# One core, a recurrent kernel with a four-stage tail: the reciprocal of the gate sum is taken over a product of two batches

## The reference, cut to what matters

```python
forget_gate = sigmoid(x @ W_f.T + b_f)
input_gate  = sigmoid(x @ W_i.T + b_i)
gate_sum    = forget_gate + input_gate + 1e-8
forget_norm = forget_gate / gate_sum
input_norm  = input_gate / gate_sum
new_info    = input_norm * (x @ W_h.T + b_h)
log_ret     = log(forget_norm + 1e-8)          # then a cumulative product over time,
hidden      = ...                              # and two cumulative sums that use it
```

## Time and profile before

| | |
|---|---|
| runs shown | 985.35, 986.1, 988.47 us, median 986.1 |
| the profiled execution | span 989.0 us (the page gives no other time of it) |
| PE busy | 943.0 us, 95% of the span |
| PEld busy | 766.4 us, 77% |
| DVE busy | 802.5 us, 81%, of which the reciprocal of the gate sum 107.3 us (32 of 3353 ns) |
| ACT busy | 647.3 us, 65% |
| POOL busy | 221.2 us, 22% |

### The profile page before, as it was taken

One profiled execution on the slowest core, in us unless ns is written; L12 is line 12 of the kernel. 1 busy time (PEld: TensorE's weight loads), 2 busy tenths in 40 slices (PEclk: granted clock), 3 DMA queues, 4 the chain that ended last, 5 costly groups with the idle time before them and its releaser, 6 DMA issues.

```text
span 989.0 us, 112546 instructions
## 1 busy us (share of the span) xinstructions
PE 943.0 (95%) x50966; PEld 766.4 (77%) x50966; DVE 802.5 (81%) x2372; ACT 647.3 (65%) x2862; POOL 221.2 (22%) x430
## 2 busy tenths in 40 slices
PE   6699999999999999999999999969999999999996
PEld 5699999999999999999999998335555555555554
DVE  2378778878788778777878787799999999999992
ACT  2478777777777777777777776336455556555552
POOL 0011111111111111111111111324434334434340
PEclk7699999999999999999999999979999999999998
DMA  6113312310010100100101001100011000001001
GB/s 218 41 55 112 110 50 95 111 35 27 24 37 24 37 24 27 34 27 24 37 24 37 24 27 33 28 1 25 24 37 34 24 24 24 24 31 41 24 24 43
DMA packets 38294, 42.01 MB, mean 42 GB/s; under 512 B 5120, under 2 KB 31232, under 8 KB 37120
## 3 DMA queue, kind: packets, MB, share of 16 engines
q1 hardware_dynamic: 36832, 40.55, 13.2%
q10 hardware_dynamic: 1440, 1.18, 0.4%
HBM read 32.80 MB, written 8.91 MB: 42 GB/s over the span
## 4 chain that ended last, share of the span: by engine, by line
PE 57%; DVE 29%; issue 7%; ACT 4%; DMA 1%; ACTq 1%; POOL 0%; DVEq 0%; POOLq 0%
PE bank L788 30%; PE bank L734 22%; DVE arena L667 10%; DVE early L686 4%; DVE early L677 4%; ACT cand_kept L391 2%; DVE early L690 2%; DVE early L684 2%; DVE early L671 2%; DVE early L665 2%; DVE none_h L604 2%; PE bank L906 2%; PE bank L923 1%; DMA bias<-in_bias 1%; PE bank L877 1%
## 5 line engine op out<-in xcount | busy, mean ns | idle before, releaser
L734 PE MATMUL bank<-x_ahead,early 128*32 128x64 f32 x12376 | 345.7, 224 | 5.9 <-ACT bank L358 3.2
L734 PEld LDWEIGHTS bank<-x_ahead,early 128*32 128x32 f32 x12376 | 239.7, 111 | 3.3 <-issue 3.3
L788 PE MATMUL bank<-none_h,early 128*32 128x32 f32 x16384 | 203.1, 199 | 8.8 <-issue 4.9
L280 POOL TENSOR_TENSOR x<-x_f,h_gx 128x64 f32 x256 | 87.6, 342 | 529.4 <-PE bank L788 528.3
L788 PEld LDWEIGHTS bank<-none_h,early 128*32 128x32 f32 x16384 | 180.6, 110 | 27.4 <-DVE none_h L604 13.5
L906 PE MATMUL bank<-x,wl 128*128 (+1 forms) x384 | 182.3, 614 | 0.9 <-DVE rank_rows L646 0.9
L788 PE MATMUL bank<-rh_f,early 128*32 128x32 f32 x8192 | 151.0, 199 | 5.0 <-DVE rh_f L592 2.2
L906 PEld LDWEIGHTS bank<-x,wl 128*128 128x128 f32 x384 | 69.2, 192 | 89.0 <-issue 89.0
L788 PEld LDWEIGHTS bank<-rh_f,early 128*32 128x32 f32 x8192 | 122.1, 112 | 7.0 <-DVE rh_f L592 5.0
L604 DVE TENSOR_TENSOR_SCAN none_h<-zero_z,cand_kept 128x64 f32<-128x64 f32 x512 | 121.6, 279 | 5.3 <-ACT cand_kept L391 3.9
L402 ACT ACTIVATE h_gx<-h_pre 128x64 f32<-128x64 f32 x256 | 68.7, 268 | 81.0 <-DVE h_pre L630 81.0
(11 more groups left out here) (95 smaller groups left out, 1294.4 us busy)
## 6 DMA issues: line engine op xcount, KB each, us to landing
x_in<-in_x SPq DMA_DIRECT2D x34, 256.0 KB, 2.7
x_ahead<-in_x SPq DMA_DIRECT2D x130, 64.0 KB, 1.8
arena<-in_w SPq DMA_DIRECT2D x8, 1024.0 KB, 5.6
out<-y SPq DMA_DIRECT2D x32, 256.0 KB, 2.5
rank_rows<-in_bias_rows SPq DMA_DIRECT2D x1, 1024.0 KB, 5.0
arena<-scratch SPq DMA_DIRECT2D x64, 16.0 KB
early<-in_cx SPq DMA_DIRECT2D x1, 768.0 KB, 4.5
early<-in_wx SPq DMA_DIRECT2D x1, 768.0 KB, 6.3
```

The costliest lines, as they stand in the source:

```text
L280: pool.tensor_tensor(x2[:, :, :, s], x1_f[:, u % LOOP], h1_gx[:, u % 2, :, :, 0], ALU.add).then_inc(x2_done, 1)
L734: mm = pe.matmul(out[32 * j:32 * j + 32], weights(k, j, m), moving(k), start=False, stop=False, tile_position=(0, 32 * j), skip_group_chec ...
L788: mm = pe.matmul(out[32 * j:32 * j + 32], weights(k, j, m), moving(k), start=False, stop=k == 1, tile_position=(0, 32 * j), skip_group_che ...
```

## The change

The reciprocal of 512 sums becomes three instructions. The sums of the two batches are multiplied with each other (256 elements), the reciprocal of the product is taken (256 elements), and that one result is multiplied with the sums again, the batches crossed over: 1/a = b * 1/(ab), and 1/b = a * 1/(ab). The last multiplication has 512 elements; it reads the sums with the two batches in reverse order, and reads the 256 inverses twice through a step of zero. Three waits of DVE on itself go between them, as there was one before.

```diff
@@ -113,6 +113,7 @@
         dec_start = sb("dec_start", [P, HALVES, GB * RUN])
+        prod, inv = [arena[2][:, 4 * COLS + n * T:4 * COLS + (n + 1) * T] for n in range(2)]
         u_s, v_s = early[:, 10 * COLS:10 * COLS + T], early[:, 10 * COLS + T:11 * COLS]
@@ -162,6 +163,7 @@
         l2_pre, f_done, i_done, c_done = sem("l2_pre"), sem("f_done"), sem("i_done"), sem("c_done")
+        prod_done, inv_done = sem("prod_done"), sem("inv_done")
@@ -664,7 +666,13 @@
                 dve.wait_ge(s_done, c + 1)
-                dve.reciprocal(rec[:, k], s_t).then_inc(rec_done, 1)
+                dve.tensor_tensor(prod, s_t[:, 0:T], s_t[:, T:COLS], ALU.mult).then_inc(prod_done, 1)
+                dve.wait_ge(prod_done, c + 1)
+                dve.reciprocal(inv, prod).then_inc(inv_done, 1)
+                dve.wait_ge(inv_done, c + 1)
+                crossed = by_batch(s_t)[:, ::-1, :]
+                both = bass.broadcast_tensor_aps(crossed, inv.rearrange("p (o t) -> p o t", o=1))[1]
+                dve.tensor_tensor(by_batch(rec[:, k]), both, crossed, ALU.mult).then_inc(rec_done, 1)
                 dve.wait_ge(rec_done, c + 1)
```

## The result

19 runs of the changed kernel took 987.25 to 992.95 us, median 991.09; 19 runs of the kernel before 985.35 to 989.35, median 986.6. The ratio is 1.0034, with a 95% interval of 1.0023 to 1.0045: 3.4 us slower, 2.3 to 4.4. One run of e5 (4792.55 us) and one of the kernel before beside it (1000.73 us) were slow and count in no ratio.

A forecast was written before the change was run, and what follows sets the result against it. PE was taken to bound the kernel at 21.26 us a phase, DVE full and in step. Start with first phase 0.6, twelve phases 1.6, lost lead 0.6 and final adapter 0.3 made +3.1: 989.2 us, range 988 to 992.

The forecast's parts named there:

- PE sets the phase and DVE's saving is worth nothing in the loop: Tail loop: PE sets 21.26 us a phase, so DVE's 0.41 us saved a unit gains nothing by itself.
- The prices of the three instructions: DVE's replacement in each unit: product of 256 at 0.43 us, reciprocal of 256 at 1.76, crossed product of 512 at 0.69.
- The pair blocks an instruction with two inputs, and which comes first behind it decides: POOL's two multiplications hold DVE's two-input instructions: the crossed product ends 0.55 us behind them, the scan starts 1.20 behind.
- The loop is 21.40 us: Loop through the engines exceeds PE's 21.26 us by 0.14; twelve such phases cost +1.6 us.
- The lost lead: End of the tail: DVE's lead over PE falls from 0.79 to 0.15 us, so the last x3 comes 0.64 later.
- The start: Start of the tail: two forget units each lose about 0.5 us net to POOL's pair, +1.0 at PE's first products.
- Half of it given back by the clock: At PE's first products, running at half clock: a microsecond less of that gives back 0.5, leaving +0.5 us.
- The final adapter: End of the kernel: PE waits longer and again starts slowly at low clock, +0.3 us, bounds -1.7 to +1.7.
- A: Rival: in the tail DVE runs ahead and the end gains, 979 to 983 us; chance 0.15.
- B: Rival: the loop closes just under PE's period, or the crossed product slips between POOL's multiplications; 987.3 us; chance 0.25.
- C: Rival: the crossed, repeated operand slows DVE's product to up to 1.4 us, 994 to 997; chance 0.12 together with D.
- D: Rival: DVE's reciprocal of 256 costs up to 3.35 us, 38 us over 32 units; chance 0.12 together with C.

The follow-up runs named there:

- e5: The kernel before, with the reciprocal taken of the first batch's 256 sums alone (work left out): 987.8 us, ratio 0.9997.
- e2: The changed kernel, with POOL's two multiplications (ic and ni) on 2 elements a partition in place of 512: 982.52 us, ratio 0.9949.
- e7: The changed kernel itself run once more, unaltered, for a second profile: 988.9 us, ratio 1.0025 to the kernel before.
- e9: The changed kernel, with six small memsets on DVE, each waited for, ahead of the first unit: 989.97 us, ratio 1.0020.
- e4: The changed kernel, with both POOL multiplications of a unit issued when the next unit's sums are ready: 989.66 us, ratio 1.0027.
- e8: The changed kernel, with the old reciprocal of 512 kept in the very first unit alone: 989.91 us, ratio 1.0024.
- e1: The kernel before, with POOL's two multiplications (ic and ni) on 2 elements a partition in place of 512: 982.41 us, ratio 0.9948.
- e3: The kernel before, with both POOL multiplications of a unit issued when the next unit's sums are ready: 981.76 us, ratio 0.9946.
- e6: The changed kernel, with only the second of POOL's two multiplications (ni) on 2 elements in place of 512: 986.34 us, ratio 0.9993.

## Why the prediction came out right, point by point

Forecast were 989.2 us, +3.1 over the median of 986.1; measured 991.09 against 986.6 in the same number of runs, ratio 1.0034 or +3.4 us (the medians, +4.5). The case in front, that the loop through PE, ACT, POOL and DVE grows past PE's own phase, is the one that happened. By its steps:

- *PE sets the phase and DVE's saving is worth nothing in the loop.* Right, and stronger than I wrote: e2 shows that the saving is worth nothing even where POOL is out of the way, and e5 that nearly four times as much is not where POOL's pair is in it.
- *The prices of the three instructions.* 0.43, 1.76 and 0.69 us against 0.42, 1.75 and 0.69 (the last in e2).
- *The pair blocks an instruction with two inputs, and which comes first behind it decides.* Right: the crossed product ends 0.54 us behind the pair, I had 0.55; L685 starts 1.19 behind, I had 1.20. By full blocking, as the prediction took it from the Trainium skill ("SBUF — State Buffer", section "Who interferes with whom"), the end would have been 0.69 behind; the rows keep some 0.14 us of overlap. The page says of two inputs that they contend, and calls the ports an exclusive lock; its words "fully blocks" stand beside DVE's 2-port modes.
- *The loop is 21.40 us.* 21.34 in the phase shown, and thirteen phases are 0.79 us longer in place of the 1.7 that I had for the loop and the first phase. This is the term that was mis-sized. Each of its links was read within 0.03 us, but what matters is the excess over 21.26, a small difference of large numbers: 0.14 forecast, 0.08 in the phase shown and 0.066 in the mean of twelve.
- *The lost lead.* 0.64 forecast, 0.72 measured. I had priced only the wait for the last x3. I had named ACT's wait for fn, but gave no term to what hangs on it: PE's second rank products come 0.73 later as well.
- *The start.* +1.0 us at PE's first products was forecast and 0.93 to 1.08 measured, but for the wrong reasons. I had each of two units lose half a microsecond to the pair. In the changed kernel the first of them loses nothing and the second 0.14; the rest, 0.94 and in e7 0.79, is the gap of 1.6 to 1.8 us before the first small reciprocal, which I had not seen coming. e9, without the gap, has the blocking that I forecast for the second unit (0.46 us).
- *Half of it given back by the clock.* The stretch behind the first rank products is 1.0 and 0.4 us shorter in the two profiles. It is not a firm term: it takes 22.66 to 23.93 us in the five profiles whose first rank products come late (the changed kernel's, e7, e4, e8, e9), and 23.71 to 24.23 in the six others.
- *The final adapter, +0.3, bounds of 1.7 either way.* Here single profiles say little. The two profiles with the change end 2.9 and 1.3 us faster than the one before; the medians say that this is chance. The stretches whose length repeats add up to 2.5 us, and 0.4 to 1.0 of that came back behind the first rank products, which leaves some 1.5 to 2.1. Where the rest of the measured 3.4 lies, the clock at the end above all or the interval of the measurement (2.3 to 4.4), isn't shown; that the sum of 3.1 came out so close is in part luck, since the phase was forecast 0.8 too dear and the gap at the start was not in it.

The rivals: that DVE runs ahead (A) is what happens without the pair or with the pair timed by DVE (e1, e2, e3), and its price was close: 979 to 983 forecast, 981.8 to 982.5 measured (5 us under the kernel before). It doesn't happen here because the crossed product is held behind the pair. The point that I named for A, M2 costing under 0.59 us behind the pair, was wrong by my own sum: 0.59 is the very value that gives the 21.40, and the loop drops under 21.26 only below 0.45. Measured are 0.58 (838.66 - 838.08), and with the measured links the point is 0.50. B, a loop just under PE's period, missed by 0.08 us. Its turned order, M2 between POOL's two multiplications, shows in the second unit of e9: M2 takes 0.73 us there, and L679 behind it is held instead (1.64). C and D are excluded by the 691 and 1753 ns.

## What to carry to other kernels

A slow instruction with one input can be the only time in which another engine works without one holding the other; before it is shortened, look at what runs beside it, and ask which instruction is the first one behind that work. Where two engines are full and in step, add up the loop that ties them, from the release of one to the release of the next, and compare it with the period: the chain of waits names the engine it stands on and not the one that sets the pace. And the gain here lay in when POOL's pair is issued, not in DVE's arithmetic: the few lines that let DVE time it make the kernel with the old reciprocal 5.3 us faster (e3), while the same lines under the short one leave it slower than before (e4).

## What the hardware showed that I had not expected

- Contention can work as a lock. In the kernel before, e5 and e6, DVE's unit settles at 10.63 us, half of PE's 21.26, without any wait on another engine noted, though its instructions would need some 10.4, 8.8 and 10.0 us if left alone (estimates: 10.63 less what the held instructions lost). The difference appears as longer durations of L671, L677 or L675 and as nothing else.
- The gap of 1.5 to 1.8 us before one instruction, in five profiles of four kernels on at least three chips, that six dummy instructions ahead of it removed. What it waits for isn't shown.
- A wait at the end can cost more than its length, and it matters where the low clock falls. With PE idle for 1.17 and 0.59 us (e3) the clock stayed at 1.00, that is 2.4 GHz. With 1.97 and 3.74 us (before) the mean fell to 0.91 over 39 us, which is some 7 us at 1.2 GHz by my estimate, and the work behind the second wait took 2.8 us more. With 2.70 and 0.96 us (changed) the low clock came as early as the first wait and was over by the second, and the work behind it took no longer than in e3 (16.4 us beside 16.5).
